# Delta stage of a two-layer kernel: three order tables in place of one, and the first head's weights loaded in the first norm

## The reference

```python
mixed = silu(causal_conv1d(h @ w_qkv, conv_w))        # 4 taps, 16 q, 16 k, 32 v heads of 128
q, k, v = split(mixed); q, k = l2norm(q), l2norm(k)
z = h @ w_z; beta = sigmoid(h @ w_b); g = -exp(A_log) * softplus(h @ w_a + dt_bias)
def step(St, (q_t, k_t, v_t, g_t, b_t)):               # per sequence and value head
    St = St * exp(g_t)
    St = St + k_t (x) ((v_t - k_t @ St) * b_t)
    return St, q_t @ St
out = (rmsnorm(core) * norm_weight * silu(z)) @ w_out
x = x + out
```

## Time and profile before

| | us |
|---|---|
| median of 3 runs (1699.21 to 1701.25) | 1699.26 |
| the profiled execution | 1702.14 |
| its span | 1700.3 |
| TensorE busy (share of the span) | 1587.0 (93%) |
| VectorE busy | 1216.5 (72%) |
| GpSimd busy | 908.4 (53%) |
| ScalarE busy | 860.2 (51%) |

### The profile page before, as it was taken

One profiled execution on the slowest core, in us unless ns is written; L12 is line 12 of the kernel. 1 busy time (PEld: TensorE's weight loads), 2 busy tenths in 40 slices (PEclk: granted clock), 3 DMA queues, 4 the chain that ended last, 5 costly groups with the idle time before them and its releaser, 6 DMA issues. The chain is left out here.

```text
span 1700.3 us, 28667 instructions
## 1 busy us (share of the span) xinstructions
PE 1587.0 (93%) x9280; PEld 1168.9 (69%) x9280; DVE 1216.5 (72%) x2565; ACT 860.2 (51%) x2367; POOL 908.4 (53%) x1101
## 2 busy tenths in 40 slices
...
DMA packets 128642, 82.58 MB, mean 49 GB/s; under 512 B 92304, under 2 KB 110992, under 8 KB 128368
## 3 DMA queue, kind: packets, MB, share of 16 engines
...
q10 hardware_dynamic: 1088, 1.05, 0.2%
...
## 5 line engine op out<-in xcount | busy, mean ns | idle before, releaser
L926 DVE SCALAR_TENSOR_TENSOR dr_acc<-dr_raw,dr_wh,dr_acc 128x512 f32<-128x512 f32 x384 | 363.5, 960 | 46.1 <-ACT dr_acc L792 42.1
L1138 PE MATMUL dr_pp<-xnT,dr_wh 128*128 128x512 f32 x512 | 243.5, 609 | 6.0 <-DMA dr_wh<-in_w_head 5.4
L1138 PEld LDWEIGHTS dr_pp<-xnT,dr_wh 128*128 128x128 f32 x512 | 93.1, 194 | 88.6 <-issue 72.1
L1218 PEld LDWEIGHTS dr_pI<-dr_V,dr_X 128*64 128x64 f32 (+1 forms) x1536 | 125.3, 156 | 40.4 <-issue 30.5
L717 POOL TENSOR_TENSOR dr_dT<-dr_rows,dr_hs 128x512 f32<-128x512 f32 x64 | 76.5, 1195 | 134.2 <-issue 119.6
L1200 PEld LDWEIGHTS dr_pI<-dr_Y,dr_nl 128*64 128x64 f32 (+1 forms) x1536 | 125.5, 156 | 17.9 <-issue 13.5
L1170 PE MATMUL dr_pp<-dr_wh,xnT 128*128 128x256 f32 x512 | 124.5, 387 | 12.6 <-DVE x L1118 6.6
L1218 PE MATMUL dr_pI<-dr_V,dr_X 128*64 128x64 f32 (+1 forms) x1536 | 134.5, 242 | 0.2 <-DVE dr_V L1056 0.2
L1200 PE MATMUL dr_pI<-dr_Y,dr_nl 128*64 128x64 f32 (+1 forms) x1536 | 132.4, 240 | 1.7 <-DMA dr_Y<-dr_blocks_y 1.5
L791 ACT ACTIVATE dr_raw<-dr_pp 128x512 f32<-128x512 f32 x128 | 75.9, 593 | 107.2 <-PE dr_pp L1138 68.1
L1290 PE MATMUL dr_pp<-dr_wo,xn 128*128 128x256 f32 x512 | 124.3, 386 | 3.6 <-issue 1.8
...
## 6 DMA issues: line engine op xcount, KB each, us to landing
...
dr_blocks_l<-dr_nl SPq DMA_DIRECT2D x128, 16.0 KB, 1.7
```

What stands on the lines that cost most here:

```text
L926: dve.scalar_tensor_tensor(acc[q][:], raw[q][:, w:w + S], wh[at.ps][:, col:col + 1], acc[q][:], ALU.mult, ALU.add).then_inc(done[q], 1)
L1138: mm = pe.matmul(flat(ps), wh[at.ps][:, w0:w0 + P], k.xnT[:, kt, b * S:(b + 1) * S], start=(kt == 0), stop=(kt == KT - 1))
L1218: mm = pe.matmul(pairs(h, s)[rows, u].rearrange("p m s -> p (m s)"), left[:, h * HU + u], V[h][:, u], start=True, stop=True)
```

## The change

1. PRO, WINDOW and LAST are three tables of their own, with the same steps as before each, in other orders. `turns` and TURN_STAGES go. In WINDOW `yz` goes from between gap1 and gap2 to the front, conv2 goes ahead of v0, v1 ahead of y0, y3 next to y4, tapb2 and tapc2 ahead of m2, project_r1 ahead of lane8, gate1 and vals2 ahead of project2. In PRO both sums of the queries go ahead of dexp0, `yz` goes behind am2, and at2 and the taps of conv4 and conv7 ahead of the lanes. In LAST core2 goes ahead of project1, recallq2 and core0 ahead of solve2, and v5 behind solve0.
2. The order tables were made with the changes of operand width on TensorE counted; no code but the tables shows this.
3. The load of the first head's weights goes from the delta stage into the first norm, behind the gate tensors and ahead of router0 and bias0, with a tensor `wh0` and a semaphore that live from there on.
4. `summing` takes the order of the sums from PRO in the prologue.

```diff
@@ phase_norm
+                sp.dma_start(k.wh0[:], w_head_dram[0]).then_inc(k.s_wh0, 16)
                 sp.dma_start(k.router0[:], router_dram.rearrange("(k p) e -> p k e", p=P)).then_inc(k.s_router0, 16)
...
+PRO = """
+row0 conv1 scal conv_r1 conv0 conv_r0 tapa1 tapb1 tapc1 conv3 silu1 tapa0 row1 tapb0 tapc0 gap0 conv2 conv_r3 row2
+tapa3 silu0 conv_r2 tapb3 gap1 row3 tapc3 tapa2 queries1 gap2 queries0 qsq1 silu3 qsq0 tapb2 keys1 keys_r1 tapc2
+silu2 keys0 gram0 gram1 ksq1 keys_r0 ksq0 gap3 dexp0 dexp1 nscal gate3 conv5 mt0 mt1 dexp2 conv_r5 gate_r3 at0 at1
+cm0 gram2 tapa5 dexp3 cm1 mt2 nl0 gram3 conv4 cm2 nl1 mt3 nl2 conv_r4 cm3 nl3 am0 tapb5 gate0 tapc5 tapa4 conv7
+gate_r0 silu5 am1 at2 tapb4 conv_r7 gath tapc4 tapa7 gathr conv6 silu4 tapb7 vals0 tapc7 conv_r6 gate1 tapa6
+vals_r0 lane0 lane1 lane2 lane3 lane4 lane5 gate_r1 gate2 lane6 vals1 silu7 lane7 gate_r2 lane8 lane9 lane10 lane11
+am2 lane12 putx yl tapb6 tapc6 silu6 puty vals3 vals_r1 vals_r3 yz vals2 vals_r2 at3 scaty scatx am3
+""".split()
 WINDOW = """
-conv1 row0 scal conv_r1 row1 conv0 gap0 conv_r0 tapa1 tapb1 tapc1 tapa0 conv3 tapb0 gap1 v0 silu1 conv_r3 m0 row2
-tapc0 silu0 conv2 conv_r2 tapa3 dexp0 y0 tapb3 queries0 a0 qsq0 tapc3 xa0 v1 tapa2 v2 dexp1 m2 conv5 y2 row3 m1 y1
-yz tapb2 tapc2 silu3 a2 silu2 v4 keys0 xb0 gram0 conv_r5 m4 queries1 keys_r0 ksq0 a1 y4 mt0 v3 gram1 a4 solve0 qsq1
...
-recall3 project_r0 lane1 lane2 recallq3 core1 core_r1 gate0 rhs3 am0 solve3 lane3 lane4 factor2 qs3 lane5 project1
-dl3 output3 oz2 lane6 lane7 gate_r0 lane8 corev2 lane9 core2 project_r1 o3 oz3 lane10 gate2 lane11 core_r2 square3
-lane12 at2 gate_r2 project2 factor3 corev3 gate1 yl tapc7 putx puty project_r2 vals2 gate_r1 silu7 at3 core3
-vals_r2 vals3 am1 vals_r3 core_r3 project3 scaty am2 project_r3 scatx am3
+row0 conv1 yz scal conv_r1 conv0 conv3 gap0 tapa1 conv_r0 tapb1 tapc1 silu1 conv2 tapa0 conv_r3 v0 tapb0 row1 tapc0
+v1 tapa3 silu0 m0 conv_r2 tapb3 m1 queries0 dexp0 tapc3 tapa2 y0 y1 a0 row2 gap1 silu3 tapb2 gap2 qsq0 xa0 tapc2 v2
+silu2 m2 conv5 a1 y2 xa1 row3 conv_r5 queries1 gap3 tapa5 a2 qsq1 v3 v4 m3 keys1 m4 keys0 gram0 xb0 y4 dexp1
...
+core_r0 tapc7 gate_r0 lane0 square2 lane1 project0 rhs3 core1 recallq3 factor2 oz2 lane2 lane3 project_r0 lane4
+solve3 core_r1 lane5 lane6 lane7 qs3 dl3 project1 silu6 output3 corev2 project_r1 lane8 core2 core_r2 o3 lane9
+lane10 am1 oz3 gate2 square3 gate_r2 lane11 factor3 gate1 vals2 gate_r1 project2 corev3 lane12 yl vals_r2 silu7
+puty project_r2 core3 am2 vals3 at3 putx scaty core_r3 project3 vals_r3 scatx project_r3 am3
+""".split()
+LAST = """
+v0 v1 m0 m1 y0 a0 y1 xa0 v2 a1 m2 y2 a2 v4 v3 xb0 xa1 m3 m4 y4 a4 y3 a3 solve0 dl0 ds0 v5 output0 update0 o0
+square0 m5 st0 recall1 rhs1 xb1 solve1 y5 dl1 ds1 recallq1 a5 update1 oz0 factor0 corev0 qs1 output1 st1 recall2 o1
+rhs2 recallq2 square1 core0 core_r0 solve2 project0 dl2 oz1 project_r0 ds2 update2 factor1 qs2 st2 output2 recall3
+corev1 o2 core1 oz2 rhs3 square2 factor2 core_r1 recallq3 solve3 qs3 dl3 corev2 output3 o3 core2 square3 project1
+project_r1 core_r2 oz3 project2 factor3 corev3 core3 project_r2 core_r3 project3 project_r3
 """.split()
...
-PRO = [x for x in WINDOW if not turns(x)]
-LAST = [x for x in WINDOW if turns(x)]
...
-        wh = [sb(f"wh{i}", [P, WROW]) for i in range(2)]
+        wh = [k.wh0, sb("wh1", [P, WROW])]
...
-            load_w(w_head_dram[0:1], 0)
             load_w(w_head_dram[1:2], 1)
...
-                order = [n for n in WINDOW if stem(n) in ("ksq", "qsq")]
+                order = [n for n in (PRO if at.kind == "pro" else WINDOW) if stem(n) in ("ksq", "qsq")]
```

More of the change, by code:

```diff
@@ L114, in __init__ @@
                                                      for n in ("gates", "router0", "rows"))
+        self.s_wh0 = ctx.enter_context(nc.semaphore("dr_w0"))
         self.rows_dram = nc.dram_tensor("gt_rows", [HK, CH, U * P], F32).ap()
@@ L141, in phase_norm @@
         if load:
-            x_dram, cst_dram, w_ab_dram, dt_bias_dram, a_log_dram, router_dram, bias_dram = load
+            x_dram, cst_dram, w_ab_dram, dt_bias_dram, a_log_dram, router_dram, bias_dram, w_head_dram = load
             @block.sync
@@ L331, in _ @@
             dve.tensor_tensor(sc[:, :, BETAV, :], sc[:, :, BETA, :], emlo[:], ALU.mult).then_inc(beta_ready, 1)
-WINDOW = """
-conv1 row0 scal conv_r1 row1 conv0 gap0 conv_r0 tapa1 tapb1 tapc1 tapa0 conv3 tapb0 gap1 v0 silu1 conv_r3 m0 row2
-tapc0 silu0 conv2 conv_r2 tapa3 dexp0 y0 tapb3 queries0 a0 qsq0 tapc3 xa0 v1 tapa2 v2 dexp1 m2 conv5 y2 row3 m1 y1
-yz tapb2 tapc2 silu3 a2 silu2 v4 keys0 xb0 gram0 conv_r5 m4 queries1 keys_r0 ksq0 a1 y4 mt0 v3 gram1 a4 solve0 qsq1
-tapa5 keys1 conv4 gap2 tapb5 xa1 mt1 dl0 at0 gap3 m3 ds0 tapc5 y3 keys_r1 at1 update0 ksq1 output0 st0 silu5 gram2
@@ L339 @@
-o0 conv_r4 a3 tapa4 recall1 v5 recallq1 dexp2 rhs1 solve1 nscal tapb4 mt2 cm0 xb1 m5 cm1 square0 nl0 tapc4 dl1
-dexp3 conv6 gram3 ds1 qs1 mt3 cm2 nl1 y5 update1 silu4 output1 a5 oz0 conv7 st1 cm3 nl2 factor0 conv_r6 nl3 conv_r7
-recall2 gate3 o1 square1 rhs2 solve2 tapa7 gate_r3 vals0 dl2 corev0 ds2 vals1 recallq2 tapa6 vals_r0 tapb6 qs2
-tapb7 core0 oz1 gath factor1 vals_r1 update2 output2 tapc6 core_r0 silu6 st2 o2 project0 corev1 square2 gathr lane0
-recall3 project_r0 lane1 lane2 recallq3 core1 core_r1 gate0 rhs3 am0 solve3 lane3 lane4 factor2 qs3 lane5 project1
@@ new lines @@
+""".split()
+WINDOW = """
+row0 conv1 yz scal conv_r1 conv0 conv3 gap0 tapa1 conv_r0 tapb1 tapc1 silu1 conv2 tapa0 conv_r3 v0 tapb0 row1 tapc0
+v1 tapa3 silu0 m0 conv_r2 tapb3 m1 queries0 dexp0 tapc3 tapa2 y0 y1 a0 row2 gap1 silu3 tapb2 gap2 qsq0 xa0 tapc2 v2
+silu2 m2 conv5 a1 y2 xa1 row3 conv_r5 queries1 gap3 tapa5 a2 qsq1 v3 v4 m3 keys1 m4 keys0 gram0 xb0 y4 dexp1
+keys_r1 y3 a4 keys_r0 ksq1 gram1 mt0 tapb5 at0 solve0 dl0 ds0 mt1 conv4 at1 ksq0 a3 output0 dexp2 tapc5 update0
+gram2 dexp3 gram3 o0 conv_r4 nscal st0 cm0 xb1 silu5 cm1 recall1 tapa4 v5 recallq1 rhs1 mt2 tapb4 solve1 m5 y5 nl0
```

13 lines of the change are left out of this document (6 added, 7 removed).

## The result

| | before | after |
|---|---|---|
| median (lowest to highest), us | 1700.26 (1699.21 to 1702.35), 4 runs | 1741.58 (1736.81 to 1745.67), 4 runs |
| ratio to before, 95% interval | 1 | 1.024 (1.021 to 1.027) |
| profiled execution, its span, us | 1702.14, 1700.3 | 1742.15, 1740.4 |

The forecast was 1685.8, range 1672 to 1698: wrong in sign and in range. Table by stage of the changed kernel (start:end, length, busy us and instructions of TensorE, weight loads, VectorE, ScalarE, GpSimd, clock, DMA share, GB/s): prologue, a full head, last head, as the earlier trace rows.

A forecast was written before the change was run, and what follows sets the result against it. Full windows were taken as bound by TensorE's work and the gaps between its groups, prologue and end of last head by chains. Prologue -7.5, windows -6, last head 0 made -13.5 us: 1685.8, range 1672 to 1698.

The forecast's parts named there:

- What bounds the kernel: Full windows bound by TensorE's work and what stands between its groups; prologue and end of last head by chains.
- Windows, -0.4 each: 15 full windows: visit -0.3, tail -0.8, wait at y2 +0.7, together -0.4 us each, -6 us in all.
- The visit, -0.3: Inverse in full windows: one visit less of 64-wide groups among 128-wide ones on TensorE saves 0.3 us per window.
- rival 4: Windows: one narrow visit less gives nothing, only the load's 4.6 us remain, about 1695 us; chance 0.08.
- The tail, -0.8: Window's tail, project1 to project3: project_r1 ahead of lane8 and fewer steps ahead of rhs3 take 0.8 us off.
- The wait at y2, +0.7: Window's head: all twelve taps ahead of m2 make y2 or v2 wait, taken as +0.7 us per window.
- my slower rival: Window's head: wait at y2 passes 1.6 us, windows +0.8 to +1.2, about 1706 us; chance 0.07.
- Prologue, -7.5: Prologue of the delta stage: early load and new order of its steps together save 7.5 us, bounds -4.6 to -11.
- Last head, 0: Last head: longer wait for the scatter of Y offset by filled waits, sum 0, bounds -3 and +3 us.

The follow-up runs named there:

- e1_load: Kernel before with only the early load of the first head's weights, all three order tables old; 1693.99 us, ratio 0.995 to before.
- e2_oldwin: Changed kernel with the old WINDOW table put back, new PRO, new LAST and early load kept; 1697.74 us, ratio 0.996 to before.
- e3_newwin: Changed kernel with old PRO and old LAST, new WINDOW and early load kept; 1740.95 us, ratio 1.023 to before.
- e9_restored: e6_cover with st1 ahead of nl1, am0 behind ds2, at2 behind lane12 and tapa6 behind rhs2; 1746.31 us, ratio 1.026 to before.
- e6_cover: Changed kernel with keys1 and y3 put back behind solve0 in the window; 1729.65 us, ratio 1.014 to before.
- e16_products: e11_st1 with keys1 and y3 ahead of solve0, as the changed kernel has them; 1739.61 us, ratio 1.019 to before.
- e11_st1: e9_restored with st1 moved behind nl1 on VectorE, as in the old window; 1726.71 us, ratio 1.012 to before.
- e13_oldback: e6_cover with VectorE and GpSimd in the old window's order behind solve0, TensorE's order staying new; 1810.79 us, ratio 1.059.
- e14_oldback_pe: Changed kernel with VectorE and GpSimd in the old order behind solve0, keys1 and y3 staying ahead of it; 1799.87 us, ratio 1.056.

## Why the prediction was wrong

- **What bounds the kernel: the first step that failed.** I wrote that the 15 full windows are bound by TensorE's own work and what stands between its groups. The table by stage had VectorE at 60.0 of 70.5 us, and I took the mean for slack. By stretches it is 18.57 of 20.75, then 6.83 of 6.83, and rhs2 ends only 0.4 us before solve2: from solve0 to recall3 the chains over VectorE and GpSimd are almost as long as TensorE's work, and in the changed kernel TensorE waits for them.
- **Windows, -0.4 each: +3.0.** The sum had three terms, at the visit, the tail and y2. The stretch between solve0 and recall3 had none; I took its chains (ds1, st1, rhs2, corev0) as unchanged, though the tables move keys1 and y3 out of it and at2 and tapa6 ahead of rhs2. There 2.4 of the 3.0 us are lost: 1.66 and 0.79. As y3's visit left the first stretch too, what TensorE waits there has grown by 1.96.
- **The visit, -0.3: its price held.** The slots give 0.3, and there are 6 instead of 7; the gain itself no run shows alone. The Trainium skill ("TensorE: Matmul & The Clock Gate", "Architectural detail: the array is 16× 32×32, not 1× 128×128"), by whose rule I made rival 4, says that weight loads are pulled ahead of running products; the rows of the changed kernel again show 0.3 us lost per visit at a change of width. What I left out is the price of bringing the groups together.
- **The tail, -0.8: +0.3.** gate2 still waits (0.70 with its refill), since project_r1 stands earlier in VectorE's order but VectorE itself is later. project2 waits 0.25 (0.35 forecast), vals3 nothing (0.45 forecast), but core3 0.32 and project3 0.38, for which I had no term.
- **The wait at y2, +0.7: +0.2.** This was my term against and my slower rival. The place was right, the size was not: in three of fourteen windows v2 waits 0.53 to 0.55 us for a0 and y2 then 0.19 for m2, in the others the taps are done in time or up to 0.17 late. The whole stretch from conv1 to solve0 loses 0.3 more than before. The main loss is elsewhere.
- **Prologue, -7.5: -6.5** (conv1 of window 0 at 95.41, before 101.91), with the gates' first sums at 36.90 instead of 33.37, 3.5 us late. The load alone gives as much: e1_load has that conv1 at 95.30, with the first sums at 34.82. I had the gain of the load too small: conv1 didn't only start without its 5.4 us wait, it ran faster (below). The new PRO, to which I gave 3 us of the 7.5, gave nothing over the old one in this pair (e2_oldwin 95.54): nscal came at 62.62 instead of 65.14, but the first lane at 86.44 instead of 85.98, behind the nine taps that now stand ahead of it. Over all traces it may be worth up to 1 or 2 us: from the first sums to that conv1 pass 58.5 to 60.8 us in the twelve traces with the new PRO, 60.5 and 62.1 in e1_load and e3_newwin with the old.

The 16 products of conv1 in the changed kernel and the start of window 0; then the wait before the last head:

```profile
42.67 7.10 PE L1144 MATMUL dr_pp<-xnT,wh 128*128 128x512 f32 x16 [0.73 <-PEq L211]
...
95.41 1.92 PE L1144 MATMUL dr_pp<-xnT,dr_wh 128*128 128x512 f32 x2
...
1202.94 2.36 PE L1206 MATMUL dr_pI<-dr_Y,dr_nl 128*128 128x64 f32 x16 [2.46 <-DMA dr_Y<-dr_blocks_y]
```

- **Last head, 0: +3.7** with the last window. The wait for dr_Y is 2.46 (3 forecast, 1.54 before). With old windows the new LAST shows no cost: from the last solve0 but one to the stage's last product pass 109.0 us in e1_load and 108.5 in e2_oldwin. With the new window single traces don't settle it: 113.4 in the changed kernel and 110.4 with the old LAST (e3_newwin), but 109.6 to 116.4 in the other traces with the new one, with granted clocks of 0.93 (after), 1.00 (e3_newwin) and 0.81 (e9_restored, 116.4) between the last v0 and solve0.
- **Chances.** 0.82 for faster rested on a sum in which each term was a wait that I could see. A wait that doesn't exist yet has no row; "slower" had 0.07 and one mechanism, and the true one wasn't among the rivals.

**What is shown and what stays open.** Shown: the new WINDOW table is the loss (e2_oldwin, e3_newwin). The place of keys1 and y3 is 0.76 to 0.91 us of the 3.0 (e6_cover against after, e16_products against e11_st1). Put back alone, that brings 0.9; with four steps of VectorE and GpSimd put back too, the waits only change their place. The other 2 us stay open: they lie in the rest of the new WINDOW. That they belong to VectorE's and GpSimd's order is likely from what TensorE waits for, but not shown; no single step was found that carries them, e13_oldback and e14_oldback_pe, which were to decide it, lost more elsewhere, and the old order of TensorE with the new one of the others was not run. That contention between the two engines is part of it is argued, not shown: VectorE is busy for 61.8 us a window after and 60.1 before for the same steps, GpSimd for 53.4 and 50.7.
